# An int4 attention layer with a mixed feed-forward part: v from plain codes, rescaled between four quarters; q's sine product on all 128 lanes, its halves swapped by transfers within SBUF; a new order of instructions

## The chip, the cores and the metric

One core of a Trainium2 chip runs one program. The metric is the device time of the program in microseconds (us); lower is better. The engines are TensorE (PE, with its weight loads, PEld), VectorE (DVE), ScalarE (ACT), GpSimd (POOL) and SyncE (SP), which issues every transfer.

## The reference, cut to what matters

```python
h = conv(x, weight) + c @ c_weight.T + bias              # 128 sequences x 32 tokens, 512 features
q, k, v = h @ dequant(q), h @ dequant(k), h @ dequant(v) # dequant: (codes - 8) * scale, one scale per 128 input rows
q, k = rope(q), rope(k)                                  # 32 q heads share 8 kv heads, 128 wide
out = softmax(mask(q @ k.T) * scale) @ v @ dequant(o)
x = x + out
x = x + ffn(cond2(x))                                    # mixing, base product, top-2 of 28 LoRA experts
```

The inner size is 512, so each column of a projection has four scales, one for each group of 128 input rows.

## The kernel before

A first block prepares tables and convolves; then `attention_and_ffn` runs 64 steps: 8 kv heads, and for each head 8 chunks of 512 tokens (4096 tokens in all). After the last step comes the feed-forward tail. All orders are written out by hand: each engine has a function `body(n, i, p, r)` that issues its part of one turn of the loop, where `n` is the step whose projections are made, `i = n - 1` the step whose scores and softmax are made, `p = n - 2` the step whose values and output are made, and `r = n - 3` an older one that finishes. Semaphores alone tie the engines together.

The stages of a step, with the names that the prediction uses:

- **q**: `project_q(n, tile, kt)` for four tiles (heads) and four quarters `kt` of the inner size. The weights are bare codes in fp16 and the activations are two fp16 parts (`hp`), so a quarter is two matmuls of 512 columns. Between two quarters ACT multiplies the PSUM bank by the ratio of their scales (`scale_q`), so that the running sum is always in units of the next quarter's scale. The last scale is folded in the rope tables.
- **rope of q**, in two pairs of tiles: DVE multiplies the PSUM banks by the cosine table into `q_f` (`turn_cos`) and by the sine table into `q_sin` (`turn_sin`), the latter in two operations of 64 lanes that read the other half of the partitions; POOL adds the two (`add_q`).
- **k**: the same in bank 7 (`kv_bank`), rescaled by DVE (`scale_k`), moved out by ACT (`move_k`) and rotated on POOL (`rotate_k_sin`, `rotate_k_cos`, `add_k`).
- **v**: `project_v` in bank 7 too, after `move_k`. Its weights can't be rescaled per partition, since tokens lie on the partitions here, so POOL prepares two fp16 parts of the scaled weight (`make_f`, `make_v_high`, `make_v_low`), and each product takes three passes (`PASSES`): 48 matmuls of 128 columns a step. ACT moves the result out (`move_v`), and POOL splits it in two parts (`v_high`, `v_low`).
- **scores**, then `scores_T`, `softmax_max` (DVE), `shift` (POOL), `exp` (ACT), `softmax_sum`, `softmax_inverse` (DVE), `normalize` (POOL), `softmax_T` (DVE), `p_high`, `p_low` (POOL).
- **values** in banks 4, 5, 6 and 1, split by `out_high` (ACT) and `out_low` (DVE); **output** in banks 4 and 5 with `scale_o` (ACT) between quarters, added to `accT` by `add_out` (DVE).

Below, q30 stands for `project_q` of tile 3, quarter 0, and so on; o00 for `output` of tile 0, quarter 0.

## Time and profile before

| | |
|---|---|
| median of 3 runs | 1615.27 us (1615.13 to 1615.29) |
| the profiled execution | 1617.53 us, span 1615.7 us |
| busy: PE | 1597.1 us, 99% of the span |
| DVE | 1399.0 us, 87% |
| ACT | 1231.1 us, 76% |
| POOL | 1127.9 us, 70% |
| mean granted TensorE clock | 0.997 |

The span is what one execution took by the profiler; the run's own time is 1.8 us longer. PE counts as busy while a matmul is under way, and its matmuls overlap. That all of PE is busy doesn't say that it never waits for another engine in a step.

### The profile page before, as it was taken

To read this page: it belongs to the slowest core of one execution; us is meant where nothing else is said; L and a number is where in the kernel's file an instruction comes from. 1 tells how busy PE (TensorE), PEld (TensorE's weight loads), DVE (VectorE), ACT (ScalarE), POOL (GpSimd) and SP (SyncE) were. 2 spreads that over 40 slices of the span, in tenths; PEclk is the share of its full clock that TensorE was granted. 3 is DMA by queue.
4 is the path that set the end of the run, shared out by engine and by line. 5 is a ranking of instruction groups with operands and counts; after the bars stand their busy time and mean duration, and the time that the engine had idled before them with its cause. 6 is when DMAs were issued, how large, how long until landed. Compare 5 with 4: busy or idle time off the path is not lost.

```text
span 1615.7 us, 36744 instructions
## 1 busy us (share of the span) xinstructions
PE 1597.1 (99%) x14878; PEld 894.6 (55%) x14878; DVE 1399.0 (87%) x2176; ACT 1231.1 (76%) x2158; POOL 1127.9 (70%) x942
## 2 busy tenths in 40 slices
PE   9989999999999999999999999999999999899999
PEld 8845555555555555555555555555555555566665
DVE  5868888888888888888888888888888888888887
ACT  3458888888888888888888888888888888532222
POOL 1168877877787778777877787778787787623332
PEclk9999999999999999999999999999999999999999
DMA  8400010001000100010001000100000012122221
GB/s 303 136 25 15 14 34 15 14 15 34 15 14 14 34 14 15 14 34 14 14 15 34 14 15 15 34 14 15 15 2 28 26 11 83 34 72 80 79 82 50
DMA packets 32312, 60.77 MB, mean 38 GB/s; under 512 B 11512, under 2 KB 14392, under 8 KB 31888
## 3 DMA queue, kind: packets, MB, share of 16 engines
q1 hardware_dynamic: 32144, 58.42, 11.3%
q8 instruction: 119, 1.95, 0.5%
q14 instruction: 49, 0.40, 0.1%
HBM read 47.46 MB, written 10.95 MB: 36 GB/s over the span
## 4 chain that ended last, share of the span: by engine, by line
PE 92%; DVE 2%; POOL 1%; issue 0%; ACT 0%; POOLq 0%; DVEq 0%
PE banks L844 27%; PE banks L761 27%; PE banks L786 11%; PE banks L775 7%; PE banks L900 5%; PE banks L804 4%; PE banks L828 3%; PE banks L943 2%; PE banks L885 2%; PE banks L871 1%; PE banks L858 1%; POOL q_f L1408 1%; DVE q_sin L1136 0%; PE banks L934 0%; POOL k_f L1392 0%
## 5 line engine op out<-in xcount | busy, mean ns | idle before, releaser
L1530 ACT ACTIVATE banks<-banks,ratios 128x512 f32<-128x512 f32 x768 | 495.4, 676 | 119.9 <-PE banks L761 110.2
L761 PE MATMUL banks<-hT,w_q 128*128 128x512 f16 x2048 | 571.3, 380 | 7.4 <-DVE q_sin L1136 3.6
L844 PE MATMUL banks<-o_hl,w_o 128*128 128x512 f16 x2048 | 567.4, 379 | 0.6 <-DVE accT L1198 0.6
L1540 ACT ACTIVATE banks<-banks,ratios 128x512 f32<-128x512 f32 x768 | 479.4, 670 | 35.1 <-PE banks L844 35.0
L1408 POOL TENSOR_TENSOR q_f<-q_f,q_sin 128x1024 f32<-128x1024 f32 x128 | 301.7, 2357 | 68.6 <-DVE q_sin L1136 59.1
L844 PEld LDWEIGHTS banks<-o_hl,w_o 128*128 128x128 f16 x2048 | 187.0, 98 | 245.5 <-ACT banks L1540 50.4
L1136 DVE TENSOR_TENSOR q_sin<-banks,rope_q 64x1024 f32<-64x1024 f32 x256 | 312.8, 1222 | 8.1 <-POOL q_f L1408 2.4
L761 PEld LDWEIGHTS banks<-hT,w_q 128*128 128x128 f16 x2048 | 184.7, 98 | 236.0 <-DVE q_sin L1136 22.7
L786 PE MATMUL banks<-w_v,hT 128*128 128x128 f16 x3072 | 196.1, 221 | 0.0
L1129 DVE TENSOR_SCALAR banks<-banks,ratios 128x512 f32<-128x512 f32 x192 | 145.2, 756 | 56.7 <-PE banks L775 56.7
L786 PEld LDWEIGHTS banks<-w_v,hT 128*128 128x128 f16 x3072 | 180.1, 99 | 22.1 <-issue 0.7
L1392 POOL TENSOR_TENSOR k_f<-k_f,rope_k 64x512 f32<-64x512 f32 x128 | 162.3, 1268 | 14.5 <-POOL q_f L1408 10.7
L1198 DVE SCALAR_TENSOR_TENSOR accT<-banks,scales,accT 128x512 f32<-128x512 f32 x224 | 157.6, 745 | 9.4 <-PE banks L844 3.8
L1189 DVE TENSOR_TENSOR o_hl<-banks,o_hl 128x512 f16<-128x512 f32 x256 | 159.2, 684 | 2.9 <-ACT o_hl L1545 0.9
L1136 DVE TENSOR_TENSOR q_f<-banks,rope_q 128x1024 f32<-128x1024 f32 x128 | 154.1, 1204 | 3.6 <-PE banks L761 1.5
L775 PE MATMUL banks<-hT,w_k 128*128 128x512 f16 x512 | 152.8, 380 | 0.0
L1545 ACT ACTIVATE o_hl<-banks 128x512 f16<-128x512 f32 x256 | 132.3, 604 | 17.8 <-PE banks L828 17.8
L1412 POOL TENSOR_TENSOR sc<-sc,stats 128x512 f32<-128x512 f32 x64 | 67.0, 1047 | 103.3 <-DVE stats L1169 103.3
L1417 POOL TENSOR_TENSOR sc<-sc,stats 128x512 f32<-128x512 f32 x64 | 67.1, 1048 | 93.3 <-DVE stats L1177 93.3
L1156 DVE STREAM_TRANSPOSE sc<-banks 128x512 f32<-128x512 f32 x64 | 45.9, 717 | 74.4 <-PE banks L804 74.4
L1478 POOL TENSOR_TENSOR w_q<-hT,w_q 128x512 f16<-128x512 f32 x32 | 37.1, 1159 | 77.0 <-ACT w_q L1560 77.0
L900 PE MATMUL banks<-hT,w_o 128*128 128x512 f16 x372 | 85.4, 379 | 0.0
(131 smaller groups left out, 1930.0 us busy)
## 6 DMA issues: line engine op xcount, KB each, us to landing
codes<-in_codes SPq DMA_DIRECT2D x40, 512.0 KB, 3.7
accT<-in_xT SPq DMA_DIRECT2D x16, 512.0 KB, 9.7
hT<-in_x SPq DMA_DIRECT2D x32, 256.0 KB, 2.8
out<-codes SPq DMA_DIRECT2D x31, 256.0 KB, 2.0
v_s<-in_v_scales SPq DMA_DIRECT2D x8, 256.0 KB, 4.5
hT<-aggb_rows SPq DMA_DIRECT2D x1, 2048.0 KB, 7.1
f_src<-in_base_T SPq DMA_DIRECT2D x4, 256.0 KB, 9.6
base_rows<-f_hl SPq DMA_DIRECT2D x4, 256.0 KB, 3.2
```

The costliest lines, as they stand in the source:

```text
L761: mm = pe.matmul(banks[:, tile], w.q[:, n[2], kt * RF * HD + tile * HD:kt * RF * HD + (tile + 1) * HD], hT[:, n[1], kt, hp], start=kt == 0 ...
L775: mm = pe.matmul(kv_bank, w.k[:, n[2], kt * HD:(kt + 1) * HD], hT[:, n[1], kt, hp], start=kt == 0 and hp == 0, stop=hp == 1, skip_group_ch ...
L786: mm = pe.matmul(kv_bank[:, j * HD:(j + 1) * HD], hT[:, n[1], kt, hp, j * P:(j + 1) * P], w.v[:, n[2], wp, kt * HD:(kt + 1) * HD], start=m ...
L844: mm = pe.matmul(o_bank(tile), w.o[:, p[2], h * D + tile * P:h * D + (tile + 1) * P], o_hl[:, op, h], start=h == 0 and op == 0, stop=op == ...
L900: pe.matmul(base_bank(t), y_hl[:, t % 2, yp, k * P:(k + 1) * P], base[:, wp, k], start=i == 0, stop=False, skip_group_check=True)
L1136: return dve.tensor_tensor(dst.rearrange("p t (b s) -> p t b s", s=S), q, t, ALU.mult)
L1189: dve.tensor_tensor(lo, pv_bank(p, b).rearrange("p (j h q) -> p j h q", h=RF, q=S), hi, ALU.subtract).then_inc(out_ready[b], 1)
L1198: ins = dve.scalar_tensor_tensor(out=dst, in0=o_bank(tile), scalar=last, in1=dst, op0=ALU.mult, op1=ALU.add)
L1392: ins = pool.tensor_tensor(by_s(k_f[64 * h:64 * (h + 1), 1]), by_s(k_f[src, 0]), table(w.rope_k[:, n[2], 1], src), ALU.mult)
L1408: pool.tensor_tensor(q, q, q_sin[:], ALU.add).then_inc(q_ready[pair], 1)
L1530: act.activation(banks[:, tile], banks[:, tile], ACT.Copy, scale=w.ratios[:, n[0], tile, kt:kt + 1]).then_inc(q_scaled[tile], 1)
L1540: act.activation(o_bank(tile), o_bank(tile), ACT.Copy, scale=w.ratios[:, p[0], RF + tile, h:h + 1]).then_inc(o_scaled[tile], 1)
```

## The change

- **v by plain codes.** k's and v's codes become one fp16 tensor `w.kv` in one POOL operation (`make_kv`), in place of five that made k's, the scaled v's and its two parts. `project_v(n, kt)` now multiplies one quarter in two passes: 8 matmuls of 128 columns, 32 a step. Between quarters DVE multiplies the bank by a table of ratios (`scale_v`, quarters 0 to 2), and the last `scale_v` multiplies by the last scale and writes `v_f`, in place of ACT's `move_v`. The table has one value per column, the same on all partitions: the first block computes it (six small DVE operations, one transpose, one copy), stores it to DRAM (`vt_rows`), and SP loads it for each head.
- **q's sine product.** One operation of 128 lanes writes `q_sin`, unswapped. SP then issues two transfers of 64 partitions each (`swap`), which write `q_sw` with the halves exchanged; `add_q` reads `q_sw`. `turn_sin` waits for the swap of the other pair instead of for `add_q`.
- **Order.** `turn_sin` comes ahead of `turn_cos`. Three quarters of v are made at the end of the turn in which q and k are made, the last one in the next. `output` of tile 2, quarter 3 and its two `add_out` move back to their own turn, so nothing is left for `r`. On POOL `rotate_k_sin` moves ahead, between `normalize` and `p_high`, and `add_q` of pair 1 moves behind `add_k`. SP's transfers of weights stand between the swaps.

```diff
+    def make_kv(self, pool, g):
         self.wait_piece(pool, g, 0)
-        pool.tensor_scalar(self.k[:, g % 2], self.codes[:, 0, 0:KT * HD], -8.0, 1.0, ALU.add, ALU.mult)
-    (make_f, make_v_high, make_v_low)
+        pool.tensor_scalar(self.kv[:, g % 2], self.codes[:, 0], -8.0, 1.0, ALU.add, ALU.mult).then_inc(self.piece_done, 1)
...
+        def swap(n, pair):
+            sp.wait_ge(q_sin_done[pair], at(n) + 1)
+            if pair or at(n):
+                sp.wait_ge(q_ready[1 - pair], at(n) + pair)
+            for h in range(2):
+                sp.dma_start(q_sw[64 * h:64 * (h + 1)], q_sin[64 * (1 - h):64 * (2 - h)]).then_inc(q_swapped[pair], 16)
+        def body(n, i, p, r):
+            if i:
+                swap(i, 1)
+            if i:
+                load_weights(i)
+                load_ffn(i)
+            if n:
+                swap(n, 0)
...
-        def project_v(n, half):
-            if half == 0:
+        def project_v(n, kt):
+            if kt:
+                pe.wait_ge(v_scaled, 3 * at(n) + kt)
+            else:
                 pe.wait_ge(k_moved, at(n) + 1)
-            for j in (2 * half, 2 * half + 1):
-                for kt in range(KT):
-                    for hp, wp in PASSES:
-                        mm = pe.matmul(kv_bank[:, j * HD:(j + 1) * HD], hT[:, n[1], kt, hp, j * P:(j + 1) * P],
-                                       w.v[:, n[2], wp, kt * HD:(kt + 1) * HD], start=m == 0, stop=m == 3 * KT - 1)
+            for j in range(CT):
+                for hp in range(2):
+                    mm = pe.matmul(kv_bank[:, j * HD:(j + 1) * HD], hT[:, n[1], kt, hp, j * P:(j + 1) * P],
+                                   w.kv[:, n[2], (KT + kt) * HD:(KT + kt + 1) * HD], start=kt == 0 and j == 0 and hp == 0,
+                                   stop=hp == 1, skip_group_check=True)
...
         def turn_sin(n, pair):
+            wait_q(n, pair)
             if pair or at(n):
-                dve.wait_ge(q_ready[1 - pair], at(n) + pair)
-            for h in range(2):
-                ins = turn(n, pair, 1, slice(64 * (1 - h), 64 * (2 - h)), q_sin[64 * h:64 * (h + 1)])
-            ins.then_inc(q_sin_done[pair], 1)
+                dve.wait_ge(q_swapped[1 - pair], 32 * (at(n) + pair))
+            turn(n, pair, 1, q_sin[:]).then_inc(q_sin_done[pair], 1)
+        def scale_v(n, kt):
+            dve.wait_ge(v_psum, KT * at(n) + kt + 1)
+            v = kv_bank.rearrange("p (j d) -> p j d", d=HD)
+            table = w.v_table[:, n[2], kt].unsqueeze(1).broadcast_to([P, CT, HD])
+            if kt < KT - 1:
+                dve.tensor_tensor(v, v, table, ALU.mult).then_inc(v_scaled, 1)
+            else:
+                dve.tensor_tensor(v_f[:], v, table, ALU.mult).then_inc(v_moved, 1)
...
         def add_q(n, pair):
-            pool.wait_ge(q_sin_done[pair], at(n) + 1)
+            pool.wait_ge(q_swapped[pair], 32 * (at(n) + 1))
+            pool.wait_ge(q_cos_done[pair], at(n) + 1)
-            pool.tensor_tensor(q, q, q_sin[:], ALU.add).then_inc(q_ready[pair], 1)
+            pool.tensor_tensor(q, q, q_sw[:], ALU.add).then_inc(q_ready[pair], 1)
...
-        def move_v(n):
-            act.activation(v_f[:].rearrange("p j d -> p (j d)"), kv_bank, ACT.Copy, scale=1 / WSCALE).then_inc(v_moved, 1)
```

The `body` functions of all engines are the tables of the new order. On DVE, about a third into the loop, these rows run from one step's last softmax operation to the mask. Before:

```order
L1177 RECIPROCAL stats<-stats 128x16
L1136 TENSOR_TENSOR q_f<-banks,rope_q 128x1024
L1184 STREAM_TRANSPOSE pT<-sc 128x512
L1136 TENSOR_TENSOR q_sin<-banks,rope_q 64x1024 x2
L1136 TENSOR_TENSOR q_f<-banks,rope_q 128x1024
L1198 SCALAR_TENSOR_TENSOR accT<-banks,scales,accT 128x512 x2
L1136 TENSOR_TENSOR q_sin<-banks,rope_q 64x1024 x2
L1189 TENSOR_TENSOR o_hl<-banks,o_hl 128x4x4x32 x4
L1165 CAST banks<-mask_b 128x512
```

and of the changed kernel, from `turn_sin(n, 0)` to the last three `out_low`:

```order
L1207 TENSOR_TENSOR q_sin<-banks,rope_q 128x1024
L1234 TENSOR_TENSOR banks<-banks,v_table 128x512
L1270 STREAM_TRANSPOSE pT<-sc 128x512
L1207 TENSOR_TENSOR q_f<-banks,rope_q 128x1024
L1234 TENSOR_TENSOR banks<-banks,v_table 128x512
L1282 TENSOR_SCALAR accT<-banks,scales 128x512 x2
L1234 TENSOR_TENSOR banks<-banks,v_table 128x512
L1207 TENSOR_TENSOR q_sin<-banks,rope_q 128x1024
L1207 TENSOR_TENSOR q_f<-banks,rope_q 128x1024
L1275 TENSOR_TENSOR o_hl<-banks,o_hl 128x4x4x32
L1238 TENSOR_TENSOR v_f<-banks,v_table 128x512
L1275 TENSOR_TENSOR o_hl<-banks,o_hl 128x4x4x32 x3
```

Four operations of 64 lanes became two of 128, four `scale_v` joined them, and the last q products of a step stand first in the next turn with only two `add_out` and a `scale_v` ahead of them.

On PE these rows are the start of a turn. Before (the first row is q00, the second o23 of step `r`, the fifth the values, the seventh q02, q30 and q10):

```order
L761 MATMUL banks<-hT,w_q 128x512 x2
L844 MATMUL banks<-o_hl,w_o 128x512 x2
L786 MATMUL banks<-w_v,hT 128x128 x24
L761 MATMUL banks<-hT,w_q 128x512 x2
L828 MATMUL banks<-pT_hl,v_hl 128x128 x48
L786 MATMUL banks<-w_v,hT 128x128 x24
L761 MATMUL banks<-hT,w_q 128x512 x6
L775 MATMUL banks<-hT,w_k 128x512 x2
```

and of the changed kernel, from the third quarter of v (its second row holds q33 and q23 of the turn that ends and q00 of the next; the row behind the last v is q30, q02, q10, q20):

```order
L854 MATMUL banks<-w_kv,hT 128x128 x8
L829 MATMUL banks<-hT,w_q 128x512 x6
L896 MATMUL banks<-pT_hl,v_hl 128x128 x48
L829 MATMUL banks<-hT,w_q 128x512 x2
L854 MATMUL banks<-w_kv,hT 128x128 x8
L829 MATMUL banks<-hT,w_q 128x512 x8
L843 MATMUL banks<-hT,w_kv 128x512 x2
```

Between q23 and q30 PE now has q00, the values, q01 and 8 small matmuls; it had q00, o23, the values, q01, q02 and 48 small ones.

On POOL, a turn of a step from `normalize` on. Before:

```order
L1417 TENSOR_TENSOR sc<-sc,stats 128x512
L1436 TENSOR_TENSOR v_hl<-v_f,v_hl 128x512
L1425 CAST pT_hl<-pT 128x512
L1440 TENSOR_TENSOR pT_hl<-pT,pT_hl 128x512
L1408 TENSOR_TENSOR q_f<-q_f,q_sin 128x1024
L1392 TENSOR_TENSOR k_f<-k_f,rope_k 64x512 x2
L1408 TENSOR_TENSOR q_f<-q_f,q_sin 128x1024
L1397 TENSOR_TENSOR k_f<-k_f,rope_k 128x512
L1401 TENSOR_TENSOR k_f<-k_f 128x512
```

and now:

```order
L1514 TENSOR_TENSOR sc<-sc,stats 128x512
L1488 TENSOR_TENSOR k_f<-k_f,rope_k 64x512 x2
L1524 CAST pT_hl<-pT 128x512
L1539 TENSOR_TENSOR pT_hl<-pT,pT_hl 128x512
L1505 TENSOR_TENSOR q_f<-q_f,q_sw 128x1024
L1493 TENSOR_TENSOR k_f<-k_f,rope_k 128x512
L1497 TENSOR_TENSOR k_f<-k_f 128x512
L1505 TENSOR_TENSOR q_f<-q_f,q_sw 128x1024
L1531 CAST v_hl<-v_f 128x512
```

The sine part of k moved ahead of the split of the probabilities, and the second `add_q`, which waits for a swap, is the last operation ahead of the scores.

## Rows read from the trace of the kernel before

**Rows 1.** The page's first part, PE.

```profile
PE 1597.1 (99%) x14878; PEld 894.6 (55%) x14878; DVE 1399.0 (87%) x2176; ACT 1231.1 (76%) x2158; POOL 1127.9 (70%) x942
```

**Rows 2.** Timeline of DVE, four turns: start us, us, instruction, idle before, releaser.

```profile
815.64 0.69 DVE L1169 TENSOR_REDUCE stats<-sc 128x16 f32<-128x512 f32 x1
...
885.03 1.23 DVE L1136 TENSOR_TENSOR q_f<-banks,rope_q 128x1024 f32<-128x1024 f32 x1
886.18 1.40 DVE L1198 SCALAR_TENSOR_TENSOR accT<-banks,scales,accT 128x512 f32<-128x512 f32 x2
...
890.10 2.48 DVE L1189 TENSOR_TENSOR o_hl<-banks,o_hl 128x512 f16<-128x512 f32 x4
892.50 0.69 DVE L1165 CAST banks<-mask_b 128x512 f32<-128x512 bf16 x1
...
894.73 0.76 DVE L1129 TENSOR_SCALAR banks<-banks,ratios 128x512 f32<-128x512 f32 x1 [0.89 <-PE banks L775]
896.63 0.72 DVE L1156 STREAM_TRANSPOSE sc<-banks 128x512 f32<-128x512 f32 x1 [1.14 <-PE banks L804]
897.38 0.69 DVE L1169 TENSOR_REDUCE stats<-sc 128x16 f32<-128x512 f32 x1
898.01 0.76 DVE L1129 TENSOR_SCALAR banks<-banks,ratios 128x512 f32<-128x512 f32 x1
...
900.20 0.68 DVE L1173 TENSOR_REDUCE stats<-sc 128x16 f32<-128x512 f32 x1
```

**Rows 3.** Timeline of PE in one turn.

```profile
887.31 0.59 PE L761 MATMUL banks<-hT,w_q 128*128 128x512 f16 x2
887.83 0.85 PE L828 MATMUL banks<-pT_hl,v_hl 32*128 32x128 f16 x48
888.62 1.51 PE L786 MATMUL banks<-w_v,hT 128*128 128x128 f16 x24
889.97 1.56 PE L761 MATMUL banks<-hT,w_q 128*128 128x512 f16 x6
...
896.50 1.04 PE L844 MATMUL banks<-o_hl,w_o 128*128 128x512 f16 x4
897.37 0.59 PE L775 MATMUL banks<-hT,w_k 128*128 128x512 f16 x2
```

**Rows 4.** Groups of DVE by shape, whole span: busy us, mean ns, idle before.

```profile
L1136 DVE TENSOR_TENSOR q_sin<-banks,rope_q 64x1024 f32<-64x1024 f32 x256 | 312.8, 1222 | 8.1 <-POOL q_f L1408 2.4
...
L1129 DVE TENSOR_SCALAR banks<-banks,ratios 128x512 f32<-128x512 f32 x192 | 145.2, 756 | 56.7 <-PE banks L775 56.7
...
L401 DVE TENSOR_TENSOR h_f<-banks,ctx_sb 128x512 f32<-128x512 f32 x32 | 22.1, 689 | 12.9 <-PE banks L337 12.2 <-PE banks L333 0.2
```

**Rows 5.** Timeline at the loop's start: a PE wait that DVE ended.

```profile
105.28 2.46 DVE L1136 TENSOR_TENSOR q_sin<-banks,rope_q 64x1024 f32<-64x1024 f32 x2
...
107.80 0.60 PE L761 MATMUL banks<-hT,w_q 128*128 128x512 f16 x2 [1.99 <-DVE q_sin L1136]
```

**Rows 6.** Timeline of POOL in one turn.

```profile
882.83 0.60 POOL L1425 CAST pT_hl<-pT 128x512 f16<-128x512 f32 x1
883.51 1.16 POOL L1440 TENSOR_TENSOR pT_hl<-pT,pT_hl 128x512 f16<-128x512 f32 x1
885.08 2.36 POOL L1408 TENSOR_TENSOR q_f<-q_f,q_sin 128x1024 f32<-128x1024 f32 x1 [0.41 <-DVE q_sin L1136]
887.62 2.59 POOL L1392 TENSOR_TENSOR k_f<-k_f,rope_k 64x512 f32<-64x512 f32 x2 [0.17 <-POOL q_f L1408]
...
901.24 1.05 POOL L1417 TENSOR_TENSOR sc<-sc,stats 128x512 f32<-128x512 f32 x1 [1.49 <-DVE stats L1177]
```

**Rows 7.** Transfers by line: count, KB each, median us to landing.

```profile
codes<-in_codes SPq DMA_DIRECT2D x40, 512.0 KB, 3.7
...
out<-codes SPq DMA_DIRECT2D x31, 256.0 KB, 2.0
v_s<-in_v_scales SPq DMA_DIRECT2D x8, 256.0 KB, 4.5
```

More of the change, by code:

```diff
@@ L545, in attention_and_ffn @@
     q_sin = sb("q_sin", [P, 2, CHUNK])
+    q_sw = sb("q_sw", [P, 2, CHUNK])
     k_f = sb("k_f", [P, 2, CHUNK])
@@ L693, in _ @@
     def _(sp):
-        for g in range(1, NKV):
-            for j in range(PIECES):
-                w.load_piece(sp, a, g, j)
         def wait_chunk(ch):
@@ L726, in _ @@
                              rows.aggw[:, h].rearrange("(t b) (i o) -> b i t o", b=TB, i=S)[b]).then_inc(mixw_loaded, 16)
-        wait_chunk(5)
-        sp.dma_start(aggb, rows.aggb.rearrange("b s -> (b s)").partition_broadcast(P)).then_inc(aggb_loaded, 16)
+        w.load_v_table(sp, rows, 0)
+        for j in range(2):
+            w.load_piece(sp, a, 1, j)
+        def body(n, i, p, r):
[6 more added lines that the diff above has]
+                swap(n, 0)
+        swap(FIRST, 0)
+        program(body)
+        swap(LAST, 1)
         wait_chunk(6)
@@ L836, in output @@
             else:
-                if tile == (1 if p not in (PRIOR, LAST) else 0):
+                if tile == 0:
                     for b in (0, 2, 1, 3):
@@ L1129, in scale_k, with turn, wait_q @@
             dve.tensor_scalar(kv_bank, kv_bank, w.ratios[:, n[0], K_ROW, kt:kt + 1], None, ALU.mult).then_inc(k_scaled, 1)
-        def turn(n, pair, which, src, dst):
-            n_parts = src.stop - src.start
-            t = w.rope_q[src, n[2], which, 2 * pair:2 * pair + 2].unsqueeze(2).broadcast_to([n_parts, 2, CHUNK // S, S])
-            q = banks[src, 2 * pair:2 * pair + 2].rearrange("p t (b s) -> p t b s", s=S)
+        def turn(n, pair, which, dst):
+            t = w.rope_q[:, n[2], which, 2 * pair:2 * pair + 2].unsqueeze(2).broadcast_to([P, 2, CHUNK // S, S])
+            q = banks[:, 2 * pair:2 * pair + 2].rearrange("p t (b s) -> p t b s", s=S)
             return dve.tensor_tensor(dst.rearrange("p t (b s) -> p t b s", s=S), q, t, ALU.mult)
-        def turn_cos(n, pair):
-            for tile in (0, 1) if pair == 0 else (3, 2):
+        def wait_q(n, pair):
+            for tile in ((1, 0), (2, 3))[pair]:
                 dve.wait_ge(q_psum[tile], KT * at(n) + KT)
@@ L1268, in body @@
             if i:
+                turn_sin(i, 1)
                 turn_cos(i, 1)
-            if r:
-                add_out(r, 2)
-                add_out(r, 3)
-            if i:
-                turn_sin(i, 1)
             if p:
                 out_low(p, 3)
+            if i:
+                scale_v(i, KT - 1)
+            if p:
                 out_low(p, 1)
@@ L1279, in body @@
                 out_low(p, 0)
+            if n:
+                scale_k(n, 0)
             if i:
@@ L1282, in body @@
             if n:
-                scale_k(n, 0)
                 scale_k(n, 1)
@@ L1290, in body @@
             if p:
+                add_out(p, 0)
                 add_out(p, 1)
-                add_out(p, 0)
             if i:
@@ L1296, in body @@
             if n:
-                turn_cos(n, 0)
+                turn_sin(n, 0)
+                scale_v(n, 0)
             if i:
@@ L1300, in body @@
             if n:
-                turn_sin(n, 0)
+                turn_cos(n, 0)
+                scale_v(n, 1)
+            if p:
+                add_out(p, 2)
+                add_out(p, 3)
+            if n:
+                scale_v(n, 2)
         scale_k(FIRST, 0)
@@ L1306, in _ @@
         scale_k(FIRST, 2)
+        turn_sin(FIRST, 0)
+        scale_v(FIRST, 0)
         turn_cos(FIRST, 0)
-        turn_sin(FIRST, 0)
+        scale_v(FIRST, 1)
+        scale_v(FIRST, 2)
         program(body)
+        turn_sin(LAST, 1)
         turn_cos(LAST, 1)
-        add_out(BEFORE, 2)
-        add_out(BEFORE, 3)
-        turn_sin(LAST, 1)
         out_low(PRIOR, 3)
+        scale_v(LAST, KT - 1)
         out_low(PRIOR, 1)
@@ L1485, in body @@
             if i:
-                rotate_k_sin(i)
-                add_q(i, 1)
                 rotate_k_cos(i)
                 add_k(i)
+                add_q(i, 1)
+                v_high(i)
                 dequantize(i)
                 shift(i)
-                v_high(i)
+                v_low(i)
                 normalize(i)
-                v_low(i)
+            if n:
+                rotate_k_sin(n)
+            if i:
                 p_high(i)
@@ L1498, in body @@
                 add_q(n, 0)
+        rotate_k_sin(FIRST)
         add_q(FIRST, 0)
         program(body)
-        rotate_k_sin(LAST)
-        add_q(LAST, 1)
         rotate_k_cos(LAST)
         add_k(LAST)
+        add_q(LAST, 1)
         x_low(0)
@@ L1576, in body @@
                 scale_q(n, 0, 0)
+            if p:
+                out_high(p, 0)
+                out_high(p, 3)
+            if n:
                 scale_q(n, 0, 1)
             if p:
-                out_high(p, 3)
-                out_high(p, 0)
                 out_high(p, 1)
                 out_high(p, 2)
-            if i:
-                move_v(i)
             if n:
```

302 lines of the change are left out of this document (169 added, 133 removed).

## The prediction

> **What bounds the kernel now.** I read the page's busy shares first: PE is busy 99% of the span, DVE 87% [rows 1]. That names PE, but a change that takes work from PE and gives some to DVE asks for more, so next I read the timeline of DVE. Four turns of the loop take from 815.64 to 897.38, 20.43 us each [rows 2]. In a turn DVE stands idle at two places only: before the second `scale_k` (0.89 us, until the product of k's second quarter is there) and before `scores_T` (1.14) [rows 2]. Between the end of the last `out_low`, 890.10 + 2.48, and `scores_T` at 896.63 lie 4.05 us [rows 2]. PE can't start o00 before the last `out_low`, and `scores_T` can't start before the scores, which stand behind six pairs of matmuls there. So this idle time isn't slack: it is PE's part of a circle out_low, output, scores, `scores_T`, and on through DVE to `out_low` again. DVE is close to binding at 87%. The kernel before has both circles nearly equal: PE's own work, and DVE with 4 us of PE in it.
>
> **What the change takes from PE.** 24 of v's matmuls take 888.62 to 889.97, 1.35 us [rows 3], 0.056 us each. 48 become 32: 0.90 us a turn less. If PE alone set the time, the turn would fall to 19.53 us.
>
> **PE's new circle.** Now `turn_sin` and `turn_cos` of pair 1 follow q23, and q30 needs the bank that both have read. From q23's start: the product of a pair of matmuls reaches its reader 0.63 us after the start (two 0.43 pairs take 896.50 to 897.37 [rows 3]; 0.2 more is my estimate for the drain, between nothing and the 0.22 by which a matmul's shown end, 0.59, and 0.06 pass the pitch of 0.43 [rows 3, 5]). Then 1.15 for the first turn (885.03 to 886.18) and 1.23 at most for the second [rows 2], and 0.06 to PE (105.28 + 2.46 = 107.74, PE at 107.80 [rows 5]): 3.05 us. PE's own work over the same way is q23 0.43, q00 with the switch to the values 0.52, the values 0.79 (887.83 to 888.62), q01 0.43 and 8 small matmuls 0.45 [rows 3]: 2.62. PE stands 0.43 us at q30 in each turn, whatever else happens. Before, 48 small matmuls and more stood there. So the turn is 19.53 + 0.43 = 19.96. To this I add 0.15 for q02, which waits for ACT's scaling of q01 behind two `out_high` (an estimate between 0 and 0.3, half of a 0.6 us ACT operation): **20.1 us**.
>
> **DVE's new circle.** Removed: four operations of 64 lanes, 4 x 1.222 [rows 4] = 4.89. Added: two of 128 lanes at 1.15 (the cosine product has the same form [rows 2]) = 2.30, and four `scale_v`. The trace has no `scale_v`. The nearest row is a product of PSUM with a broadcast float table, 128x512, 0.689 [rows 4]; back to back an operation of this size costs less, as four `out_low` take 2.40 from 890.10 to 892.50 [rows 2], 0.60 each. Below that nothing is to be had (the lanes still take 512 columns); above it stands `scale_k`, which also writes PSUM, at 0.756 [rows 4]. I take 0.61, so 2.44. DVE changes by -4.89 + 2.30 + 2.44 = -0.15, between -0.2 and +0.45. The six pairs between the first output and the scores are as many as before. Its circle goes from 20.43 at most (PE, not DVE, may have been last at its joints) to about **20.1 to 20.3**, so the 0.90 that PE saves can't be had whole.
>
> **The circle through POOL and the transfer.** It is new. From `add_q(n, 0)` the swap of pair 1 waits until `q_sw` is read, then `add_q` of pair 1, the scores and the whole softmax follow until `add_q(n, 0)` of the next turn. In order: SP's reaction 0.1 (estimate, as the 0.06 of [rows 5]); the swap, S; `add_q` 2.36 [rows 6] and 0.25 to PE and into the scores; scores to `scores_T` 1.14, as long as DVE waited for them; `scores_T` 0.75, maximum 0.63 [rows 2]; `scale_k` 0.70, two `add_out` 1.40, sum 0.71 (0.68 and the step to the next), inverse 0.25 (estimate from the 0.2 us that small operations take), all on DVE in this order [rows 2]; `normalize` with its start 1.13, `rotate_k_sin` 2.59, `p_high` 0.68, `p_low` 1.16, `add_q` 2.36 [rows 6]. `shift` and `exp` lie beside DVE's `scale_k` and `add_out`. Sum: **16.2 + S**. It fits into 20.1 while S is below 3.9, and costs the whole gain at S = 4.2. What is S? No row shows a transfer within SBUF. Below: 256 KB out of SBUF in 2.0 [rows 7], the second issued a little later, 2.4. Above: 256 KB spread over partitions in 4.5, 4.9 with the second's issue. Both halves together are 512 KB, and such a transfer of codes takes 3.7 [rows 7]. I take 3.7: the circle is 19.9 and hides below the others, narrowly. Weights for the next head are issued behind the first swap and 10 us ahead of the next, so they don't delay one.
>
> By rows this is close; the Trainium skill speaks against it more plainly. "SBUF — State Buffer", section "Can I just issue two DMAs to hit both halves?", says that two transfers on 64 partitions each run one behind the other, and its section on the port swizzle that 64 partitions reach half of the ports, 218 GB/s. By its fixed 2 us and 1.2 us for each half that would be an estimate of 4.4 us, and by it the turn would be 20.6. No run here shows either yet.
>
> **What costs nothing.** POOL loses three of five weight operations and 70% busy [rows 1] leaves room. ACT loses `move_v`. Both lie beside other engines' work; with that cover gone they are a gain, not a price. The v table is computed while the convolution runs on PE, needed only some 10 us into the loop; if it weren't hidden, it would cost one transfer, at most 4.5 us once [rows 7]. SP's weight waits name pieces that were made a turn earlier. The k path: `rotate_k_sin` now needs `normalize`, and is counted above. At the loop's ends, v's quarters of chunk 0 now stand ahead of the first full turn (24 small matmuls, 1.35 us) and 40 of 48 are gone from the last (2.25 us): -1 us, between -3 and +1.
>
> **The sum.** A turn goes from 20.43 to 20.1, -0.33; 62 full turns give -20.5; the ends -1: -21.5 us. The profiled execution took 1617.5 (span 1615.7), so 1596.0; the median of the runs before lies 2.3 below that execution, 1615.3, so **1594 us**.
>
> **The rivals.**
>
> - *DVE and PE's circle are shorter than I think* (15%). For it: the small waits of DVE before are slack that I counted as work, and ACT's 0.15 may vanish. The floor is PE's 19.96 with a drain of 0.05 less and no loss elsewhere: 19.85, -0.58 x 62 - 1 = -37: **1578**.
> - *DVE is the bound, with no gain* (12%). For it: `scale_v` writes PSUM and might take 0.70 back to back, and the two new waits for v's product sit in its circle: +0.36 over my value, so 20.4 to 20.5: **1612 to 1618**. Against: PSUM written costs nothing extra in the mask's copy, 0.69 [rows 2].
> - *The swap is the bound, and the kernel is slower* (17%). Place: `add_q` of pair 1 ends after PE has come to the scores. Price: one us a turn for each us over 3.9, 62 us in all; it decides from S = 4.2 on. At S = 4.5, the long row of [rows 7], the turn is 20.7, +0.27 x 62 - 1 = +16: **1631**. At 4.4 it is +10: 1625. For it: the row of 4.5, and two transfers where one was costed. Against: the stores of 2.0. The part of this case between 3.9 and 4.2 (a third) still ends faster, at 1596 to 1614.
> - *The change doesn't do what it says*: v's codes have 8 matmuls a quarter by the new order, so PE's saving of 0.90 is certain as work; nothing here speaks for this rival.
>
> **How the numbers follow.** The likeliest, 56%, is that three circles meet at about 20.1: 1594, its own range 1580 to 1608 (turns of 19.9 to 20.3). Measurement of this kernel can tell 0.2%, 3.2 us. Faster (below 1612): 56 + 15, 4 of the 12 and 4 of the 17, with 1 taken off my own range's edge, 78%. Same (1612 to 1618.5): 6 of DVE's case and 2 of the swap's, 9%. Slower: 13%. The range from 1573 to 1617 leaves out the slow swaps (13%) and what lies under PE's floor (4%); it takes in both bounds of `scale_v`, but not S above 4.2.
>
> **What the profile after would show.** v's matmuls 2048 in 8s; `scale_v` at 0.68 us, if 0.75 the DVE step is wrong. The turn between two maxima at 20.1. In it PE's weight load of q30 waits some 0.4 us for `q_f` of the cosine product; if not, PE's circle is wrong. The wait ahead of the scores: for `k_f` or `q_f` on POOL, behind a transfer that lands in 3.7 us; if it lands in over 4.2, POOL's `add_q` will be shown waiting for `q_sw`, PE for `add_q`, and the forecast fails on S. DVE idle ahead of the second `scale_k` and of `scores_T` as before, 0.8 and 1.14: if these are longer, the scores are late and the swap is the reason; if DVE waits elsewhere, for `out_high` or `exp`, ACT is.

## The result and the profile after

The changed kernel takes 1642.08 us (median, 1641.33 to 1646.09), the kernel before 1615.28 (1615.13 to 1616.33): the ratio is 1.017, with a 95% interval of 1.0152 to 1.0187. The forecast was 1594. The profiled execution took 1641.33, its span is 1639.5.

These are rows of the page of the changed kernel: its first part, three groups whose idle time grew, two of new work, and two kinds of transfer with their median time to landing.

```profile
PE 1555.6 (95%) x13854; PEld 831.1 (51%) x13855; DVE 1380.7 (84%) x2311; ACT 1198.0 (73%) x2094; POOL 1104.1 (67%) x910
...
L1505 POOL TENSOR_TENSOR q_f<-q_f,q_sw 128x1024 f32<-128x1024 f32 x128 | 301.3, 2354 | 125.0 <-DMA q_sw<-q_sin 125.0
...
L1207 DVE TENSOR_TENSOR q_sin<-banks,rope_q 128x1024 f32<-128x1024 f32 x128 | 153.3, 1198 | 3.0 <-PE banks L829 1.6
...
L1242 DVE STREAM_TRANSPOSE sc<-banks 128x512 f32<-128x512 f32 x64 | 45.9, 717 | 123.1 <-PE banks L871 123.1
...
L1234 DVE TENSOR_TENSOR banks<-banks,v_table 128x512 f32<-128x512 f32 x192 | 133.0, 693 | 7.9 <-PE banks L854 2.9
...
L871 PE MATMUL banks<-q_f,k_f 128*32 128x128 f32 x2048 | 69.2, 276 | 47.1 <-POOL q_f L1505 47.1
...
q_sw<-q_sin SPq DMA_DIRECT2D x256, 256.0 KB, 3.5
codes<-in_codes SPq DMA_DIRECT2D x40, 512.0 KB, 4.7
```

Every engine has less to do than in [rows 1], PE by 41.5 us and DVE by 18.3, and the span is 24 us longer. So the time went into waits. The groups name the chain: POOL's second addition waits 125.0 us for the swap, the scores 47.1 us for POOL (0.2 before), `scores_T` 123.1 us for the scores. Two of these groups before:

```profile
L1408 POOL TENSOR_TENSOR q_f<-q_f,q_sin 128x1024 f32<-128x1024 f32 x128 | 301.7, 2357 | 68.6 <-DVE q_sin L1136 59.1
...
L1156 DVE STREAM_TRANSPOSE sc<-banks 128x512 f32<-128x512 f32 x64 | 45.9, 717 | 74.4 <-PE banks L804 74.4
```

The idle time ahead of POOL alone would prove nothing, since POOL has room; that it is handed on through PE to DVE does.

One turn shows the size. Timeline of the changed kernel, POOL, SP's queue, PE and DVE:

```profile
877.92 2.37 POOL L1505 TENSOR_TENSOR q_f<-q_f,q_sw 128x1024 f32<-128x1024 f32 x1
880.37 1.10 SPq L740 DMA_DIRECT2D q_sw<-q_sin  x2
881.51 0.60 SPq L116 DMA_DIRECT2D codes<-in_codes  x1
884.75 2.34 POOL L1505 TENSOR_TENSOR q_f<-q_f,q_sw 128x1024 f32<-128x1024 f32 x1 [1.88 <-DMA q_sw<-q_sin]
887.15 1.08 PE L871 MATMUL banks<-q_f,k_f 128*32 128x128 f32 x32 [0.69 <-POOL q_f L1505]
888.30 0.72 DVE L1242 STREAM_TRANSPOSE sc<-banks 128x512 f32<-128x512 f32 x1 [1.91 <-PE banks L871]
```

`add_q` of pair 0 ends at 880.29 and frees `q_sw`; the two transfers are issued at 880.37; `add_q` of pair 1 starts at 884.75. S, as the prediction named it, is 884.75 - 880.37 = 4.4 us. DVE waits 1.91 us ahead of `scores_T` (1.14 in [rows 2]). With the prediction's 16.2 the circle is 20.6; measured from one maximum of the scores to the next, the usual turn is 20.70. From the first turn to the last the loop takes 1309.6 us against 1289.2 before, +20.4; the start is 1.8 longer and the tail 1.6.

### The profile page after: what moved, and what is told of

It is laid out like the page before. It is cut to its first block and busy times, and to the rows that moved or that the text cites. A ratio compares the mean times of both kernels' runs of the same rounds, so it can differ in the third digit from the quotient of the medians.

```text
span 1639.5 us, 35390 instructions
## 1 busy us (share of the span) xinstructions
PE 1555.6 (95%) x13854; PEld 831.1 (51%) x13855; DVE 1380.7 (84%) x2311; ACT 1198.0 (73%) x2094; POOL 1104.1 (67%) x910
## 5 line engine op out<-in xcount | busy, mean ns | idle before, releaser
L912 PE MATMUL banks<-o_hl,w_o 128*128 128x512 f16 x2048 | 575.2, 382 | 5.8 <-DVE o_hl L1275 4.0
L829 PE MATMUL banks<-hT,w_q 128*128 128x512 f16 x2048 | 550.2, 380 | 18.7 <-DVE q_f L1207 14.1
L1505 POOL TENSOR_TENSOR q_f<-q_f,q_sw 128x1024 f32<-128x1024 f32 x128 | 301.3, 2354 | 125.0 <-DMA q_sw<-q_sin 125.0
L912 PEld LDWEIGHTS banks<-o_hl,w_o 128*128 128x128 f16 x2048 | 170.9, 98 | 242.2 <-ACT banks L1635 98.3
L854 PEld LDWEIGHTS banks<-w_kv,hT 128*128 128x128 f16 x2048 | 135.3, 98 | 65.5 <-DVE banks L1234 5.2
L854 PE MATMUL banks<-w_kv,hT 128*128 128x128 f16 x2048 | 156.2, 219 | 4.5 <-DVE banks L1234 3.9
L1207 DVE TENSOR_TENSOR q_sin<-banks,rope_q 128x1024 f32<-128x1024 f32 x128 | 153.3, 1198 | 3.0 <-PE banks L829 1.6
L843 PE MATMUL banks<-hT,w_kv 128*128 128x512 f16 x512 | 152.8, 380 | 1.3 <-DVE banks L1201 1.3
L1242 DVE STREAM_TRANSPOSE sc<-banks 128x512 f32<-128x512 f32 x64 | 45.9, 717 | 123.1 <-PE banks L871 123.1
L1234 DVE TENSOR_TENSOR banks<-banks,v_table 128x512 f32<-128x512 f32 x192 | 133.0, 693 | 7.9 <-PE banks L854 2.9
L871 PE MATMUL banks<-q_f,k_f 128*32 128x128 f32 x2048 | 69.2, 276 | 47.1 <-POOL q_f L1505 47.1
```

The lines of the kernel that those rows point to most:

```text
L829: mm = pe.matmul(banks[:, tile], w.q[:, n[2], kt * RF * HD + tile * HD:kt * RF * HD + (tile + 1) * HD], hT[:, n[1], kt, hp], start=kt == 0 ...
L843: mm = pe.matmul(kv_bank, w.kv[:, n[2], kt * HD:(kt + 1) * HD], hT[:, n[1], kt, hp], start=kt == 0 and hp == 0, stop=hp == 1, skip_group_c ...
L854: mm = pe.matmul(kv_bank[:, j * HD:(j + 1) * HD], hT[:, n[1], kt, hp, j * P:(j + 1) * P], w.kv[:, n[2], (KT + kt) * HD:(KT + kt + 1) * HD] ...
L912: mm = pe.matmul(o_bank(tile), w.o[:, p[2], h * D + tile * P:h * D + (tile + 1) * P], o_hl[:, op, h], start=h == 0 and op == 0, stop=op == ...
L1207: return dve.tensor_tensor(dst.rearrange("p t (b s) -> p t b s", s=S), q, t, ALU.mult)
L1505: pool.tensor_tensor(q, q, q_sw[:], ALU.add).then_inc(q_ready[pair], 1)
```

## The experiments

Twelve kernels. "Turn" is the time between two `softmax_max` or mask operations of consecutive steps; the first and the last of the loop differ in every kernel (19.2 and 22.4 us in e1) and are left out of the column.

| kernel | median us | ratio to before, 95% interval | turn us |
|---|---|---|---|
| e1_no_swap | 1588.86 | 0.9831, 0.9809 to 0.9852 | 19.95 |
| e2_one_transfer | 1590.35 | 0.9830, 0.9807 to 0.9852 | 19.94, some 20.1 |
| e3_two_by_columns | 1594.87 | 0.9865, 0.9842 to 0.9889 | 19.95, five 20.5 to 21.4 |
| e6_every_second | 1594.11 | 0.9857, 0.9836 to 0.9878 | 19.94, five 20.3 to 21.3 |
| e10_split_swap | 1606.57 | 0.9934, 0.9917 to 0.9952 | 19.94 to 21.1 |
| e5_old_sine | 1788.15 | 1.1056, 1.1034 to 1.1078 | 22.64, some 24.3 |
| e7_half_add_out | 1588.59 | 0.9819, 0.9801 to 0.9838 | 19.95 |
| e8_half_sine | 1588.37 | 0.9828, 0.9811 to 0.9844 | 19.94 |
| x1_neighbours | 1590.76 | 0.9840, 0.9824 to 0.9857 | 19.95, three 20.4 to 20.7 |
| x2_by_tiles | 1590.08 | 0.9838, 0.9821 to 0.9854 | 19.94 |
| x3_tiles_scale_first | 1629.39 | 1.0071, 1.0053 to 1.0089 | 20.59 |
| x4_scale_first | 1628.65 | 1.0068, 1.0050 to 1.0086 | 20.59 |

### Without the swap

```diff
-            for h in range(2):
-                sp.dma_start(q_sw[64 * h:64 * (h + 1)], q_sin[64 * (1 - h):64 * (2 - h)]).then_inc(q_swapped[pair], 16)
...
-            turn(n, pair, 1, q_sin[:]).then_inc(q_sin_done[pair], 1)
+            turn(n, pair, 1, (q_sin, q_sw)[pair][:]).then_inc(q_sin_done[pair], 1)
...
-            pool.tensor_tensor(q, q, q_sw[:], ALU.add).then_inc(q_ready[pair], 1)
+            pool.tensor_tensor(q, q, (q_sin, q_sw)[pair][:], ALU.add).then_inc(q_ready[pair], 1)
```

> The changed kernel without transfers: the sine products of pair 0 and pair 1 are written into two buffers and add_q reads them as they are, so the halves of q's sine part stay unexchanged (that part of the computation is left out). Theory A (the circle through POOL and the swap sets the turn: 16.2 + 4.4 us): with the swap gone that circle is 12 us, the turn falls to what the circles of PE and DVE allow, 20.0 to 20.2 us in place of 20.7, the kernel to 1597 to 1610 us. Theory B (the new order, DVE's four scale_v and PE's wait at q30 set the turn, the swap only fills a gap): 1632 us or more.

1588.86 us, below even theory A's 1597 to 1610, since the turn is 19.95 all through and not 20.0 to 20.2. But for the transfers and their waits all of the change is in it, and it is faster than before by 1.7%. The swap costs 53 us: it turned a gain of 26 into a loss of 27.

### What about the swap is slow

Three kernels move the same 512 KB per swap in other shapes. The first two leave out the exchange of halves, the third exchanges even and odd partitions instead:

```diff
-            for h in range(2):
-                sp.dma_start(q_sw[64 * h:64 * (h + 1)], q_sin[64 * (1 - h):64 * (2 - h)]).then_inc(q_swapped[pair], 16)
+            sp.dma_start(q_sw[:], q_sin[:]).then_inc(q_swapped[pair], 32)                       # e2
+                sp.dma_start(q_sw[:, h], q_sin[:, h]).then_inc(q_swapped[pair], 16)             # e3
+                sp.dma_start(q_sw[h::2], q_sin[1 - h::2]).then_inc(q_swapped[pair], 16)         # e6
```

> The changed kernel with one transfer of 128 partitions and 512 KB in place of the two of 64 partitions; it copies without exchanging the halves (left out). Theory A1 (a transfer on 64 partitions moves at half rate, and the two run one behind the other): S falls from 4.4 to about 3.2 us, less than the 3.9 at which the circle hides, so as without any swap, within 4 us of that run. Theory A2 (the 512 KB and a fixed time make S, whatever the partitions): within 5 us of the changed kernel, 1642. Theory A3 (only the second issue counts, 0.5 us): turn 20.2, about 1612.

> The changed kernel with two transfers of 256 KB, each of all 128 partitions and one of the two tiles; no exchange of halves (left out). Theory A1 (partitions): S about 3.7, near the run without a swap, at most 8 us above it. A2 (bytes) and A3 (second issue): 1642 within 5 us.

> The changed kernel with two transfers of 64 partitions as before, but even partitions to odd ones and odd to even ones, so neighbours are exchanged instead of halves (this part of the computation is changed). Only the position of the 64 partitions differs. If it is the position (partitions of one half share half of the ports), S falls to about 3.7 and the time is within 5 us of the two transfers by columns. If it is the number of 64 or the bytes, 1642 within 5 us.

The two `add_q` of one turn, on POOL's timeline, of e2, then e3, then e6:

```profile
708.82 2.36 POOL L1504 TENSOR_TENSOR q_f<-q_f,q_sw 128x1024 f32<-128x1024 f32 x1
714.24 2.35 POOL L1504 TENSOR_TENSOR q_f<-q_f,q_sw 128x1024 f32<-128x1024 f32 x1 [0.49 <-DMA q_sw<-q_sin]
```

```profile
711.61 2.37 POOL L1505 TENSOR_TENSOR q_f<-q_f,q_sw 128x1024 f32<-128x1024 f32 x1
717.09 2.35 POOL L1505 TENSOR_TENSOR q_f<-q_f,q_sw 128x1024 f32<-128x1024 f32 x1 [0.54 <-DMA q_sw<-q_sin]
```

```profile
710.55 2.36 POOL L1505 TENSOR_TENSOR q_f<-q_f,q_sw 128x1024 f32<-128x1024 f32 x1
715.95 2.35 POOL L1505 TENSOR_TENSOR q_f<-q_f,q_sw 128x1024 f32<-128x1024 f32 x1 [0.47 <-DMA q_sw<-q_sin]
```

From the end of the first to the start of the second: 3.06, 3.11 and 3.04 us, against 4.46 (880.29 to 884.75) in the changed kernel. One transfer or two makes no difference here, so it is neither the count nor the second issue. The transfers of e6 have 64 partitions and 256 KB each, as those of the changed kernel have, and are fast: what is slow is the exchange of 64 partitions that lie in one half with those of the other. A slow half and a slow way from one half to the other can't be told apart by these runs, since no kernel copies a half onto itself. The theories with the partitions had the times right; their S of 3.7 for e3 and e6 was too high. The transfer rows of the pages, e3, then e6:

```profile
q_sw<-q_sin SPq DMA_DIRECT2D x256, 256.0 KB, 2.5
```

```profile
q_sw<-q_sin SPq DMA_DIRECT2D x256, 256.0 KB, 2.4
```

They land in 2.5 and 2.4 us where the halves take 3.5. All three kernels are back at the turn of e1; the 5 us by which e3 and e6 are over it lie in the main in five long turns each, and not in the usual one. In these the swap lands late: in e6's turn of 21.32, from 458.5 on, `add_q` waits 2.50 us for it. What holds it up there isn't settled.

The Trainium skill, "SBUF — State Buffer", section "Door 1: The DMA port swizzle (why `[64,N]` ≈ `[32,N]`)", ties the port to the partition's number so that each half of 64 has eight of the sixteen ports to itself, and every second partition reaches all sixteen; the times of e6 (3.04 us) and of the halves (4.46 us) agree. Its section "Can I just issue two DMAs to hit both halves?" says that only one transfer over all partitions reaches every port; here the two interleaved ones of e6 take no longer than the one of e2, 3.04 and 3.06 us, and the measurement decides.

With the halves kept, the swap was cut in four transfers of 128 KB, and `add_q` in two operations, so that the first can start when half of the swap has landed:

```diff
+            for t in range(2):
+                if pair or at(n):
+                    sp.wait_ge(q_ready[1 - pair], 2 * (at(n) + pair) - 1 + t)
+                for h in range(2):
+                    sp.dma_start(q_sw[64 * h:64 * (h + 1), t], q_sin[64 * (1 - h):64 * (2 - h), t]).then_inc(q_swapped[pair], 16)
```

> The changed kernel, computing the reference, with each swap in four transfers (two halves for each of the two tiles) and add_q in two operations, one for each tile: the transfers of the first tile start when add_q has read that tile, 1.2 us earlier. Theory A1 (bytes behind half of the ports, one transfer behind the other): half of the bytes are under way earlier, the last lands some 3.7 to 3.9 us after add_q in place of 4.4; turn 20.1 to 20.3, 1600 to 1615. Theory A4 (a fixed time of about 2 us for each transfer, in a row): four take longer than two, 1642 or more.

1606.57 us, within theory A1's 1600 to 1615, with turns between 19.94 and 21.1. In a turn near 700 us `add_q` of pair 0 ends at 699.38 and the first `add_q` of pair 1 starts at 702.97, 3.59 us later, where the changed kernel has 4.46. The first piece is issued at 698.39, while POOL still adds the second tile, and the last at 700.56: each piece waits only for its own half of `add_q`, so part of the swap runs beside that addition. Which of the two cuts brings more wasn't tried apart.

### The sine product in 64 lanes, no transfer

```diff
-            turn(n, pair, 1, q_sin[:]).then_inc(q_sin_done[pair], 1)
+            for h in range(2):
+                ins = turn(n, pair, 1, (q_sin, q_sw)[pair][64 * h:64 * (h + 1)], slice(64 * (1 - h), 64 * (2 - h)))
+            ins.then_inc(q_sin_done[pair], 1)
```

> The changed kernel (v by plain codes in four quarters, the new order) with q's sine product as before: two operations of 64 lanes that read the other half, no transfer, two buffers. It computes the reference. Each turn_sin costs 1.28 us more on DVE. Theory A (without the swap PE's and DVE's circles stand at 19.95 and both hold turn_sin of pair 1, DVE's also that of pair 0): the turn grows to 19.95 + 2.5 = 22.4 us, the kernel to 1589 + 63 x 2.5 = 1740 to 1750. Theory C (DVE has slack of 2 us a turn, the idle time ahead of scale_k and the scores, and takes part of it): below 1680.

1788.15 us, above both theories: this new order is slow without the 128 lanes. The usual turn is 22.64, where theory A has 22.4, and the longer ones make up most of the rest. The wait of PE in this kernel, 600 to 1100 us (total, times, longest):

```profile
PE banks L823 <- DVE q_f L1202: 42.5, 22, 2.0
```

And its windows (busy time of PE, PEld, DVE, ACT, POOL, then the granted clock, the DMA share and GB/s):

```profile
700.00:722.00 22.00, 19.38 (x147) 8.85 (x146) 19.39 (x26) 15.92 (x29) 16.27 (x13) 0.92 0.09 25
722.00:744.00 22.00, 19.38 (x183) 9.51 (x182) 19.80 (x28) 17.03 (x30) 16.28 (x13) 1.00 0.01 1
```

q30 waits 2 us for the cosine product. About one turn in four takes 24.3 us; PE's granted clock (third column from the end) is 0.92 in the window that holds one, and 1.00 in the next. Between the levels of 0.5 and 1 that mean stands for some 3.5 us at the lower one, which at half the pace costs about 1.7 us (estimate): the difference from 22.64 to 24.3.

### What holds the turn at 19.95

The prediction gave PE's circle over `turn_sin`, `turn_cos` and q30 19.96 us, and e1 measured 19.95. An agreement alone doesn't show that this circle is the limit. e7 is e1 with `add_out` of tiles 2 and 3 on half of their columns, so that half of that addition is left out; it takes work from DVE's circle. e8 is e1 with half of the sine product of pair 1 left out.

```diff
+            if tile >= 2 and p[0]:
+                dst, o = dst[:, 0:CHUNK // 2], o[:, 0:CHUNK // 2]            # e7
...
+            if pair:
+                t = w.rope_q[:, n[2], 1, 2].unsqueeze(1).broadcast_to([P, CHUNK // S, S])
+                dve.tensor_tensor(q_sw[:, 0].rearrange("p (b s) -> p b s", s=S), banks[:, 2].rearrange("p (b s) -> p b s", s=S), t, ALU.mult).then_inc(q_sin_done[1], 1)  # e8
```

> The kernel of the run without a swap, with add_out of tiles 2 and 3 on half of the columns for all heads but the first (half of that accumulation is left out, and the halves of q's sine part stay unexchanged). It takes 2 x 0.27 = 0.53 us from DVE at a place outside the way from q23 to q30. Theory P (the turn of 19.95 is PE's circle: q23, turn_sin, turn_cos, q30): 1586 to 1590. Theory D (it is DVE's circle): 1589 - 63 x 0.53 = 1555 to 1562.

> The kernel without the transfers (two buffers for the sine products, halves not exchanged), and the sine product of pair 1 on half of its columns: the exchange and that half of the sine product are left out. The row of the whole sine product is 1.20 us, half of it about 0.67. Theory P: the turn of 19.95 us of the kernel without transfers is TensorE's circle, from the last product of q tile 3 over the sine and the cosine product of pair 1 to the next product into tile 3's bank. With 0.53 us less in the circle the wait of about 0.43 goes and TensorE is held by its own work: turn 19.5 to 19.6, time 1562 to 1569. Rival Q: ScalarE or POOL, or another circle, holds the turn at 19.95, and the half product leaves it there: 1586 to 1591.

Neither moves the turn. DVE isn't the limit (e7), and the circle that the prediction had named isn't the only one (e8 was to fall to 1562 to 1569 if it were, and gave 1588.37). PE's waits between 620 and 1000 us, in e1, then in e8:

```profile
PE banks L823 <- DVE q_f L1201: 3.6, 17, 0.2
PE banks L823 <- issue: 0.5, 2, 0.3
```

```profile
PE banks L823 <- ACT banks L1624: 5.1, 19, 0.3
```

The wait for the cosine product, shown as 0.21 us a turn, is gone, and one shown as 0.27 us for `scale_q` stands in its place. This is where, in PE's and ACT's timeline of e8:

```profile
707.31 1.46 PE L823 MATMUL banks<-hT,w_q 128*128 128x512 f16 x6
708.70 0.85 PE L890 MATMUL banks<-pT_hl,v_hl 32*128 32x128 f16 x48
708.81 0.66 ACT L1624 ACTIVATE banks<-banks,ratios 128x512 f32<-128x512 f32 x1 [1.38 <-PE banks L823]
709.52 0.60 PE L823 MATMUL banks<-hT,w_q 128*128 128x512 f16 x2
709.58 1.08 ACT L1639 ACTIVATE o_hl<-banks 128x512 f16<-128x512 f32 x2
710.41 0.59 PE L823 MATMUL banks<-hT,w_q 128*128 128x512 f16 x2
710.55 0.67 ACT L1624 ACTIVATE banks<-banks,ratios 128x512 f32<-128x512 f32 x1
711.27 1.47 PE L823 MATMUL banks<-hT,w_q 128*128 128x512 f16 x6 [0.27 <-ACT banks L1624]
```

The product q01 is ready at 710.1, but its scaling stands on ACT behind two `out_high`, which wait for the values: 709.58 to 710.55. q02 needs the scaling and starts at 711.27. From the values on, ACT's two copies and one scaling take longer than PE's work beside them.

The idle time that a row shows starts at the end shown for the matmul before, which lies behind the moment at which the next one could have started: two pairs that wait for nothing start 0.43 us apart, and each is shown with 0.59. So what PE loses is read from starts. q23 is the second pair of the row at 707.31 and starts at 707.74; q30 starts at 710.41 without a wait, 2.67 us later, and q02 could follow at 710.84. It starts at 711.27: PE loses 0.43 us there. In e1 (its rows stand below) q30 starts 3.10 us behind q23, so PE loses 0.43 us at q30, and q02 follows at once, 3.53 behind q23, as in e8. The two ways, over DVE to q30 and over ACT to q02, are of the same length to within what the rows show, and with one of them shortened the other holds the turn at 19.95.

### The best version, and two ways to go on

x1 exchanges neighbours in place of halves, for k as well as for q: the columns of the weights stay in the order in which they come, the tables are interleaved, both swaps are as in e6, and POOL's two k operations of 64 lanes become one.

```diff
-                sp.dma_start(q_sw[64 * h:64 * (h + 1)], q_sin[64 * (1 - h):64 * (2 - h)]).then_inc(q_swapped[pair], 16)
+                sp.dma_start(q_sw[h::2], q_sin[1 - h::2]).then_inc(q_swapped[pair], 16)
...
+            for h in range(2):
+                sp.dma_start(sc[h::2], k_f[1 - h::2, 1]).then_inc(k_swapped, 16)
...
-        "cos2": np.concatenate([cos, cos]),
-        "sin2": np.concatenate([sin, -sin]),
+        "cos2": np.repeat(cos, 2, axis=0),
+        "sin2": np.stack([sin, -sin], axis=1).reshape(HD, S),
```

> A version meant to beat both, computing the reference: the pairs of the rotation stay neighbours (no split of even and odd columns in q, k, cosine and sine), so that the swap exchanges even and odd partitions: two transfers of 64 partitions that lie on both halves, S about 3.0. k is rotated in the same way: one POOL operation of 128 lanes writes k's sine product, two transfers exchange neighbours into the buffer sc, which is free then, and add_k adds it. POOL's circle falls by 1.3 + 1.4 us to below 18.5 and hides. Theory A: turn 19.95 as without a swap, 1587 to 1594. Theory F (more transfers on SP's queue, and SP waits for k's sine product ahead of the next swap, so the swaps come late again): 1600 or more.

1590.76 us, 1.6% faster than the kernel before and 3.1% faster than the changed one, with turns of 19.95 but for three: the swap is hidden, and the whole computation is kept. x2 adds to it that pair 1 is turned tile by tile, tile 3 first, so that q30 waits for two short operations:

```diff
-                turn_sin(i, 1)
-                turn_cos(i, 1)
+                turn_by_tiles(i)          # sine 3, cosine 3, sine 2, cosine 2
```

> The kernel with q and k in neighbouring partitions (turn 19.95), and pair 1 of q turned tile by tile: sine and cosine product of tile 3 first, so that TensorE's product into tile 3's bank waits for two operations of 512 columns (about 1.3 us) and not for two of 1024 (2.4 us). Theory P (that circle alone holds the turn at 19.95): it gets 1.0 us shorter, less what tile 2 comes later, and the turn goes to 19.6 to 19.8, time 1566 to 1580. Rival V: two more operations on VectorE, at about 0.07 us of start each, make VectorE's circle the longer one, turn 20.0 to 20.1: 1592 to 1600. Rival Q (another circle at 19.95): 1588 to 1593.

1590.08: not to be told from x1. As in e8, q30's wait is gone and the one for ACT, shown as 0.27 us, stands in its place. x3 (from x2) and x4 (from x1) then change ACT's order:

```diff
             if p:
                 out_high(p, 0)
-                out_high(p, 3)
             if n:
                 scale_q(n, 0, 1)
             if p:
+                out_high(p, 3)
                 out_high(p, 1)
```

> The half sine product and the turn tile by tile both left the turn at 19.94 us, and moved TensorE's wait from the cosine product to ScalarE: 0.27 us per turn at the product into tile 0's bank that waits for the second scaling of that bank, which stands on ScalarE behind two copies of the product of p and v. Here that scaling stands behind one copy. It can then start about 0.4 us earlier (869.95 in place of 870.35 in the trace of the tile-by-tile kernel), before TensorE is ready for it. Theory Q (this wait holds the turn): 0.27 us less per turn, turn 19.67, 63 turns, 17 us less than the 1590 of the tile-by-tile kernel: 1570 to 1577. Rival V (VectorE's circle, or the swap of pair 1 that is now nearer, holds it): the turn stays over 19.9 with a wait for VectorE or POOL in its place, 1587 to 1595.

> The kernel with q and k in neighbouring partitions, both pairs turned in whole operations, with the same change of ScalarE's order alone. Theory Q with the cosine product as the next limit: TensorE still waits 0.21 us for the cosine product of pair 1, 0.8 us of work ahead of the place where it would wait 0.27 us for ScalarE, so only the difference of 0.06 us per turn can go: turn 19.88, time 1586 to 1589 against 1590.8. If the turn falls by 0.27 us as in the other run (1570 to 1577), the cosine product is no limit at all. If it does not move (1590 to 1592) the circle over the cosine product is the limit of its own at 19.95.

Both are slower, with the same turn of 20.59, 0.65 more. All the theories missed. ACT's, PE's and DVE's timeline of x4 behind the values:

```profile
891.87 0.85 PE L906 MATMUL banks<-pT_hl,v_hl 32*128 32x128 f16 x48
891.98 0.66 ACT L1633 ACTIVATE banks<-banks,ratios 128x512 f32<-128x512 f32 x1 [1.38 <-PE banks L839]
...
892.75 0.60 ACT L1648 ACTIVATE o_hl<-banks 128x512 f16<-128x512 f32 x1
...
893.34 0.66 ACT L1633 ACTIVATE banks<-banks,ratios 128x512 f32<-128x512 f32 x1
...
893.92 1.56 ACT L1648 ACTIVATE o_hl<-banks 128x512 f16<-128x512 f32 x3
...
894.54 0.69 DVE L1285 TENSOR_TENSOR o_hl<-banks,o_hl 128x512 f16<-128x512 f32 x1 [0.65 <-ACT o_hl L1648]
...
895.38 1.02 PE L839 MATMUL banks<-hT,w_q 128*128 128x512 f16 x4 [0.36 <-DVE o_hl L1285]
```

`out_high(p, 3)` now ends near 894.5, and with it waits `out_low`, and PE with q10, the next product into the bank that both read: it starts 3.51 us behind the values, and does so in x3 too, where q30 waits for nothing. In e1 it starts 3.0 behind them. So both orders of ACT are late for someone, and they were in the better of the two. That one place in ACT's order moves the turn by 0.65 us, with either form of q's turn, speaks for this stretch, behind the values, as the limit. It isn't proved: no kernel here shortens both ways at once and makes nothing later. With both gone PE would be held by its own work; 19.95 less 0.43 gives 19.52 as an estimate of that turn, against the prediction's 19.53.

## Why the prediction was wrong

**The step that failed is the circle through POOL and the transfer.** Its form was right: the same instructions wait as it said (`add_q` for `q_sw`, the scores for `add_q`, `scores_T` for the scores), and 16.2 + S gives 20.6 where 20.70 was measured. S was mis-sized: 3.7 taken, 4.4 measured, above the 4.2 from which the swap decides. The 3.7 came from a transfer of 512 KB of codes into SBUF, over all partitions [rows 7]; e2, e3 and e6 show that the same bytes within SBUF, on partitions of both halves, need 3.0 to 3.1, and that the 1.4 us above it are due to the exchange of halves. So the row wasn't of the nearest kind: its size was that of the swap, its partitions weren't. The rival on the other side, with 1625 at 4.4, had the mechanism; 17% was too little for it. The remaining 17 us of its 1625 to 1642 are 0.1 more in the usual turn (6 us at most), ten turns of 20.9 to 22.2, and the ends. In most of the ten a swap landed late; in the one of 22.03 `add_q` waits 3.22 us for it. In the next, of 22.24, it wasn't late, but the granted clock was 0.50 from 1283 to 1286 us.

The prediction gave the estimate of 4.4 from the Trainium skill, "SBUF — State Buffer", section "Can I just issue two DMAs to hit both halves?", and a turn of 20.6 by it. The trace agrees: 4.4 and 20.70. The sum went by the row.

**PE's saving and circle.** Without the swap the turn is 19.95 against 19.96 forecast for q30's wait, and the parts are right too. PE's timeline in e1:

```profile
866.45 1.46 PE L823 MATMUL banks<-hT,w_q 128*128 128x512 f16 x6
867.85 0.85 PE L890 MATMUL banks<-pT_hl,v_hl 32*128 32x128 f16 x48
868.67 0.60 PE L823 MATMUL banks<-hT,w_q 128*128 128x512 f16 x2
869.11 0.61 PE L848 MATMUL banks<-w_kv,hT 128*128 128x128 f16 x8
869.98 1.92 PE L823 MATMUL banks<-hT,w_q 128*128 128x512 f16 x8 [0.26 <-issue]
```

q23 is the second pair of the first row and starts at 866.45 + 0.43 = 866.88. q30 starts at 869.98, 3.10 from q23, where 3.05 was forecast (its terms add up to 3.07). PE's own work over the same way is 2.67 in e8, where q30 doesn't wait, against 2.62 forecast, so the wait is 0.43, as forecast. What failed is the other term, 0.15 for q02 behind two `out_high`, and that it was added. Alone it is 0.43 from PE's own pace (e8, x2), above its bound of 0.3, and the two don't add: q30's wait lies ahead of q02 in the same stretch and takes up all of it. So 20.1 should have been 19.95. That the circle over q30 gives the measured turn by itself is in part luck: had the way over ACT been longer, it would have set the turn alone.

**DVE's circle.** `scale_v` takes 0.69 as the mean of the whole span; between two maxima DVE still has room, and taking half of two `add_out` away changes nothing (e7, 1588.59 against 1588.86). The 20.1 to 20.3 were too high; DVE's idle times were slack to that extent. Nor do they follow from the terms: 20.43 less 0.15 is 20.28, and the bounds of -0.2 and +0.45 give 20.2 to 20.9. In the same way the floor of the first rival, 19.96 with 0.05 less, would be 19.91 and not 19.85.

**The ends.** -1 was forecast, +3.4 measured. Of this, 1.8 lie ahead of the first scores, and there the kernels scatter by as much: but for e5 they reach the first `scores_T` at 99.1 to 101.0 us, against 101.0 in the changed kernel and 99.1 before. Behind the last turn PE now waits once for long, in the timeline of the changed kernel:

```profile
1403.95 2.82 PE L912 MATMUL banks<-o_hl,w_o 128*128 128x512 f16 x6 [4.02 <-DVE o_hl L1275]
```

e1 has a tail as long as the changed kernel's (228.3 and 228.2 us behind the last maximum; 226.6 before), so that part belongs to the new order and not to the swap.

**Transfers of weights.** The prediction had them cost the swaps nothing. Issued behind the first swap, they don't delay its issue, but the two slow each other: codes land in 4.7 us where they took 3.7 [rows 7], and turns without a load behind the swap take 20.56 where those with it take 20.70. Behind the interleaved swap the codes land in 3.9, behind the single transfer of e2 in 4.4 and behind the four pieces of e10 in 3.9, so it isn't the halves alone that slow them, and the cause stays open.

**What costs nothing**, POOL's weight operations, ACT's `move_v`, the v table, was so: none appears among PE's waits in the loop.

**The sum** for the rest of the change is borne out: 1594 forecast with a swap that hides, 1588.86 without a swap, 1590.76 with one that does hide.
